# Third layer of a four-layer transformer kernel: row maxima of four heads taken in four 32-row tiles of TensorE

## The chip, the cores and the metric

The kernel runs on one core of one Trainium2 chip. Its time is the device time of one launch in microseconds (us); the lower, the better. TensorE (PE) multiplies, VectorE (DVE), ScalarE (ACT) and GpSimd (POOL) work on elements, SyncE (SP) issues the DMAs. Each engine runs its own instruction list in order; semaphores tie the lists together.

## The reference

Four layers on `x` of shape (4, 1024, 256), with a residual and a layer norm around each. The change is in the third, a causal softmax attention of 16 heads of width 16, whose output is scaled per key row by a gate:

```
Q = (x @ Wq + bq).reshape(B, S, 16, 16)        # K and V likewise
logits = einsum('bqhd,bkhd->bhqk', Q, K) * 16 ** -0.5
attn = softmax(where(causal, logits, -inf))
gate = tanh(...)                                # one number for each (b, q)
out = einsum('bhqk,bkhd->bqhd', attn * gate[:, None, None, :], V) @ Wo + bo
```

(`gate[:, None, None, :]` runs over the keys.)

## The kernel before

`layer3` treats the four sequences one after the other: `projections`, `attention`, `output`. All are unrolled, and the order of the work on each engine is the order in which the Python code emits it; nothing reorders it but the waits on semaphores.

**Layout of Q and K.** `qst` and `kst` are [128, 8, 1024]. One index of the middle axis holds two heads (`a` = 0, 1), each on 64 partitions: four blocks of 16 rows. In `qst` they hold the high part of Q, its low part, nothing, the high part; in `kst` high, high, nothing, low. One product over the 64 rows thus gives hi·hi + lo·hi + hi·lo, a score close to full precision out of fp32r operands. The first row of the empty block is special: `kst` has -1 there (`krow`), and `qst` gets the row maximum of that query, so that the same product subtracts the maximum. The layout is made by matmuls with `select` in `projections`.

**Maxima first.** The maximum of a query row over its keys is needed before its scores can be exponentiated. So `attention` computes the scores twice. A *maxima tile* (list `tiles`, 96 for each sequence) is 128 queries by up to 512 keys of both heads `a` of one sub-group `u`: `maxima_part` runs one 64-row matmul for each head (L1571) into a bank each, and, where the tile touches the diagonal, two bf16 matmuls that add the causal mask (L1574, L1576). Tiles alternate between two pairs of the four banks 4 to 7; the wait `s.max_read >= i - 1` asks that tile `i - 2` was read. VectorE reduces both banks of a tile in one instruction (L1690) into `peak`, or for queries 512 to 1023, whose keys come in two halves, into `low` and `high`, which L1696 combines. SyncE then carries each column of 128 maxima into its row of `qst` by a DMA (L1559, two for each query tile).

**Scores, exponentials, values.** 48 *steps* (`steps`; one chunk of four heads and 512 queries by one key tile of 128) follow. A step has four score matmuls (`scores_part`, L1588, with two mask matmuls L1591 and L1593 on the diagonal), in the order j=0: a=0, a=1, j=1: a=0, a=1, each into one of three banks; four exponentials on ScalarE (L1678) which free those banks; and the products with V of the step two before (`weighted`, L1606, each issued as two passes). The chunks are: 0 and 1 (queries 0 to 511, four steps each), 2 to 5 (queries 512 to 1023, eight steps each), 6 and 7 (queries 0 to 511 again). Chunk c may begin when all its maxima have landed (`shifted`).

**Which maxima when.** Twelve tiles stand ahead of the first step, with the eight V projections (`value`, L1624) between them; the others are dealt out to the steps by `tiles_to`, so that each chunk's tiles are done four tiles ahead of its first step. In a step, half of its tiles go with j=0 and half with j=1, and of the first tile of each half one head's part is emitted behind each score matmul.

```
if i >= 2:
    pe.wait_ge(s.max_read, i - 1)
at = MAX + 2 * (i % 2) + a
```

## Time and profile before

| | us |
|---|---|
| runs of the kernel, median (lowest, highest) of 3 | 3317.6 (3314.07, 3318.29) |
| the profiled execution, its own time | 3319.22 |
| span of its profile | 3317.5 |
| PE busy over the span | 3158.2 (95%) |
| DVE / ACT / POOL busy | 1831.4 / 1477.7 / 1018.0 |
| attention of the third layer, four sequences, first start to end | 148.8, 144.1, 152.5, 146.6 |

The four attentions start at 1854.4, 2059.4, 2261.4 and 2470.4 us of the span. The second one (2059.4 to 2203.5) is looked at closely, since all four have the same instructions. "Busy" of PE counts a matmul from its start to its modelled end, and matmuls overlap, so a PE that is busy need not be streaming. The page's chain of what ended last is of no help here: it only covers the fourth layer.

### The profile page before, as it was taken

The numbers are of one execution on the slowest core, as the hardware profiler recorded it, in microseconds if no ns is written. First come the engines' busy times: TensorE is split into PE (matmuls) and PEld (weight loads), VectorE is DVE, ScalarE is ACT, GpSimd is POOL, SyncE is SP. The second block draws the span as 40 slices with busy tenths as digits, with TensorE's granted clock in tenths as the row PEclk, the third lists the DMA queues.
The fourth block names the chain that finished last, engine by engine and source line by source line (L and its number), as shares of the span: only waits on it lengthen the run. The fifth ranks groups of instructions, "written<-read, shape, count | busy, mean of one in ns | idle before, by whom it ended". The sixth has DMA issues, their size and how long they took to land. (4 is left out here: it accounts for less than half of the span.)

```text
span 3317.5 us, 49554 instructions
## 1 busy us (share of the span) xinstructions
PE 3158.2 (95%) x18066; PEld 2264.4 (68%) x18066; DVE 1831.4 (55%) x3090; ACT 1477.7 (45%) x2732; POOL 1018.0 (31%) x919
## 2 busy tenths in 40 slices
PE   7999999999999999999999999999999999999998
PEld 4667656975588756986578546555465588888886
DVE  4556745775467744866464665756557433333332
ACT  3332354424542254422543574655756644444443
POOL 1224424752266423753256304022040211111110
PEclk9999999999999999999999999998999999999999
DMA  6212111011121111111121001010100300000000
GB/s 204 67 39 72 33 31 56 31 47 39 30 71 39 39 28 47 39 52 34 32 61 52 2 3 51 2 27 1 9 20 2 131 25 13 13 13 14 7 7 14
DMA packets 182673, 124.07 MB, mean 37 GB/s; under 512 B 125216, under 2 KB 163360, under 8 KB 178976
## 3 DMA queue, kind: packets, MB, share of 16 engines
q1 hardware_dynamic: 182432, 120.87, 12.9%
q8 instruction: 149, 2.44, 0.3%
q14 instruction: 92, 0.75, 0.1%
HBM read 103.37 MB, written 28.44 MB: 40 GB/s over the span
## 5 line engine op out<-in xcount | busy, mean ns | idle before, releaser
L1950 PE MATMUL sums<-l_uhi,l_h 128*128 128x512 f32 x1024 | 406.3, 397 | 0.0
L1678 ACT ACTIVATE l3b_prob<-sums 128x512 f32<-128x512 f32 (+3 forms) x768 | 333.2, 493 | 160.4 <-PE sums L1593 121.7
L1950 PE MATMUL sums<-l_ulo,l_h 128*128 128x512 f32 x1024 | 403.9, 394 | 0.0
L644 POOL TENSOR_TENSOR l_qrow<-l_vm,l_qst 128x512 fp32r<-128x512 f32 x256 | 355.6, 1406 | 146.2 <-ACT l_qst L638 145.3
L1032 DVE TENSOR_REDUCE l2b_mx<-sums 128x1 fp32r<-128x1024 f32 (+7 forms) x256 | 192.6, 758 | 255.7 <-PE sums L943 254.0
L968 PE MATMUL sums<-sb_nx,l_vx 128*128 128x512 f32 (+3 forms) x768 | 302.2, 503 | 2.1 <-ACT l_od L1008 2.1
L1588 PE MATMUL sums<-l_qst,l_kst 64*128 64x512 f32 (+3 forms) x768 | 278.2, 426 | 15.6 <-ACT l3b_prob L1678 6.3
L2037 DVE TENSOR_TENSOR l_ulo<-l_made,l_uhi 128x512 fp32r<-128x512 f32 x128 | 90.4, 706 | 362.6 <-ACT l_uhi L1969 362.6
L1001 ACT ACTIVATE sb_nx<-sums 128x512 f32<-128x512 f32 (+3 forms) x384 | 182.3, 493 | 220.7 <-PE sums L960 215.4
L638 ACT CAST l_qst<-l_vm 128x512 fp32r<-128x512 f32 x256 | 158.2, 620 | 237.7 <-DVE l_vm L631 138.6
L1571 PE MATMUL sums<-l_kst,l_qst 64*128 64x512 f32 (+3 forms) x768 | 242.2, 443 | 22.2 <-DVE l3b_low L1690 11.8
L1588 PEld LDWEIGHTS sums<-l_qst,l_kst 64*128 64x128 f32 x768 | 140.2, 195 | 154.1 <-ACT l3b_prob L1678 136.5
L631 DVE TENSOR_TENSOR l_vm<-l_oT,sums 128x512 f32<-128x512 f32 x256 | 172.4, 681 | 120.6 <-PE sums L623 119.4
L1950 PEld LDWEIGHTS sums<-l_uhi,l_h 128*128 128x128 f32 x1024 | 192.9, 188 | 44.8 <-POOL l_ulo L2105 1.3
L1950 PEld LDWEIGHTS sums<-l_ulo,l_h 128*128 128x128 f32 x1024 | 193.0, 188 | 43.4
L1239 PE MATMUL sums<-l_kst,l_qst 128*128 128x256 f32 x768 | 217.5, 283 | 0.0
L2105 POOL TENSOR_TENSOR l_ulo<-l_made,l_uhi 128x512 fp32r<-128x512 f32 x64 | 82.4, 1292 | 437.7 <-ACT l_uhi L1969 437.7
L746 PE MATMUL sums<-l_kst,l_qst 128*128 128x512 f32 x512 | 208.0, 406 | 8.0 <-PEq L1107 7.4
L1996 ACT ACTIVATE l_made<-sums,l_scale 128x512 f32<-128x512 f32 x128 | 88.2, 689 | 279.3 <-PE sums L1950 279.2
L800 DVE TENSOR_TENSOR l_vm<-sums,l_gm 128x512 f32<-128x512 f32 x256 | 174.3, 689 | 66.5 <-PE sums L746 66.0
L957 PE MATMUL sums<-l_qst,l_kst 128*128 128x512 f32 (+3 forms) x384 | 206.9, 539 | 4.0 <-issue 4.0
L746 PE MATMUL sums<-l_kst,l_qrow 128*128 128x512 f32 x512 | 200.3, 391 | 0.0
(274 smaller groups left out, 7826.4 us busy)
## 6 DMA issues: line engine op xcount, KB each, us to landing
l_ve<-ve SPq DMA_DIRECT2D x32, 512.0 KB, 4.0
l_oe<-oe SPq DMA_DIRECT2D x16, 1024.0 KB, 5.0
between<-sb_x SPq DMA_DIRECT2D x48, 256.0 KB, 2.1
l_vm<-weights_copy SPq DMA_DIRECT2D x32, 352.0 KB, 3.4
sb_nx<-between SPq DMA_DIRECT2D x9, 1024.0 KB, 5.7
weights_copy<-h SPq DMA_DIRECT2D x2, 4096.0 KB, 26.1
l_ve<-inverse SPq DMA_DIRECT2D x32, 256.0 KB, 3.6
l_qst<-l3b_peak SPq DMA_DIRECT2D x512, 0.5 KB, 2.0
```

What stands on the lines that cost most here:

```text
L644: pool.tensor_tensor(rlo[:, i % RT, :], routed[:, i % RT, :], rhi[:, i % RT, :].bitcast(F32), ALU.subtract).then_inc(s3.routed_lo, 1)
L746: last = pe.matmul(bank(m.ps, n % RING), x[:, c, t * P:(t + 1) * P], v[:, h % 2, c, :], start=(c == 0 and x is xhi and v is vhi), stop=(c ...
L800: dve.tensor_tensor(by_key(vm[:, n % VM, :]), by_key(bank(m.ps, n % RING)), gm[:, at:at + NE].unsqueeze(1).to_broadcast([P, DH0, NE]), ALU ...
L957: pe.matmul(out, kst[:, h % RK, at], qst[:, h % RK, lo:hi], start=True, stop=False)
L968: last = pe.matmul(bank(m.ps, PV, lo, hi), vx[:, k, h // 2, DH0 * (h % 2):DH0 * (h % 2) + P], prob[:, k % 2, lo:hi], start=(k == 0), stop= ...
L1001: act.activation(prob[:, k % 2, lo:hi], bank(m.ps, n % 3, 0, hi - lo), ACT.Exp, scale=SCALE0).then_inc(s.exp_ready, 1)
L1032: dve.reduce_max(mx[:, h1, t:t + 1], bank(m.ps, max_bank(h1, k1), 0, (t + 1) * P), AX_X).then_inc(s.max_read, 1)
L1239: last = pe.matmul(m.ps[:, t * D:(t + 1) * D], r[:, k % RT, cols], w(c, expert(e))[:, 0, :], start=(c == e == 0 and t % 2 == 0 and r is rh ...
L1571: last = pe.matmul(bank(m.ps, at, 0, hi - lo), qst[rows(a), p, t * P:(t + 1) * P], kst[rows(a), p, lo:hi], start=True, stop=True)
L1588: last = pe.matmul(bank(m.ps, part % SCORE, 0, hi - lo), kst[rows(a), p, k * P:(k + 1) * P], qst[rows(a), p, lo:hi], start=True, stop=True)
L1678: act.activation(prob[:, i % RB, j, a, 0:hi - lo], bank(m.ps, part % SCORE, 0, hi - lo), ACT.Exp, scale=SCALE1).then_inc(s.exp_ready, 1)
L1950: run(lambda out, a, x, first, last: pe.matmul(out, a, x, start=first, stop=last))
```

## The change

It touches the third layer only.

- **Layout.** For the odd index of the middle axis the four blocks of 16 rows are rotated by two: empty, third term, first, second. So the first two terms of an even and of an odd index lie on different 32-row quarters of each head's 64 rows (0 to 31 and 32 to 63). The special row moves with them (partition 0 instead of 32; `krow` has a column for each, `spread` writes every other index).
- **Maxima.** `maxima(i)` now does tiles `i` and `i + 1` at once, the same queries and keys of an even and an odd sub-group: four matmuls (four heads), each over the 32 rows of its quarter, into banks 4, 5, 6 and 7 together. The third term (hi·lo) is left out of the maxima; the scores still have it. The subtracted number is then only nearly the maximum, which a softmax allows.
- **Masks of the maxima.** A mask now spreads over 32 rows, so a diagonal pair of tiles takes four groups of four bf16 matmuls (128, 96, 64 and 32 columns), 16 where 8 stood.
- **Waits.** `maxima(i)` waits for `s.max_read >= i`, that is, until all four banks were read.
- **Order.** `tiles` runs over a chunk's query tiles with j innermost; `tiles_to` is rounded to even numbers; a pair is emitted as a whole behind the two score matmuls of j=0 or of j=1, no longer between them. SyncE's DMAs alternate between the two sub-groups of a chunk.
- **Loads.** The mask operands grow from 3 blocks of 256 to 2 of 256 and 2 of 512 columns for each partition, once.

```diff
-        tiles = [(u, t, lo, hi) for u, (p, n) in enumerate(subs) for t in range(TPH * n, TPH * n + TPH)
-                 for lo, hi in halves(0, (t + 1) * P)]
+        tiles = [(2 * c + j, t, lo, hi) for c, (g, n) in enumerate(chunks) for t in range(TPH * n, TPH * n + TPH)
+                 for lo, hi in halves(0, (t + 1) * P) for j in range(2)]
...
-                for u, (p, n) in enumerate(subs):
-                    if u >= 2:
-                        sp.wait_ge(shifted[u % 2], carried(u - 2))
+                for c, (g, n) in enumerate(chunks):
                     for j in range(TPH):
-                        if n:
-                            sp.wait_ge(s.combined, combined_to(u, j))
...
+                        for u in (2 * c, 2 * c + 1):
...
+                def maxima(i):
+                    _u, t, lo, hi = tiles[i]
+                    if i:
+                        pe.wait_ge(s.max_read, i)
+                    ranges = [(lo, hi, None)]
                     if hi == (t + 1) * P:
...
+                        ranges += [(hi - P + q * P // QUARTERS, hi, q) for q in range(QUARTERS)]
+                    for first, end, q in ranges:
+                        for j in range(2):
+                            p = subs[tiles[i + j][0]][0]
+                            for a in range(2):
+                                quarter = slice(R * a + R // 2 * j, R * a + R // 2 * j + R // 2)
+                                out = bank(m.ps, MAX + 2 * j + a, first - lo, end - lo)
...
-                    now = list(range(tiles_to[i], tiles_to[i + 1]))
+                    now = list(range(tiles_to[i], tiles_to[i + 1], 2))
...
                             scores_part(i, j, a)
-                            if share[j]:
-                                maxima(share[j][0], a)
...
+                        for both in share[j]:
+                            maxima(both)
```

On TensorE, the first maxima ahead of the steps: `l_kst,l_qst` is the maxima matmul, `rowmask_qk` its mask, `l_wv` a V projection. Before:

```order
L1571 MATMUL sums<-l_kst,l_qst 128x128
L1574 MATMUL sums<-l_rowmask_qk,l_rowpick 128x128
L1576 MATMUL sums<-l_rowmask_qk,l_rowpick 128x64
L1571 MATMUL sums<-l_kst,l_qst 128x128
L1574 MATMUL sums<-l_rowmask_qk,l_rowpick 128x128
L1576 MATMUL sums<-l_rowmask_qk,l_rowpick 128x64
L1624 MATMUL sums<-l_wv,l_xT 128x256 x2
```

The same place in the changed kernel (`quartermask` is the mask of a quarter):

```order
L1584 MATMUL sums<-l_kst,l_qst 128x128 x4
L1587 MATMUL sums<-l_quartermask,l_quarterpick 128x128 x4
L1587 MATMUL sums<-l_quartermask,l_quarterpick 128x96 x4
L1587 MATMUL sums<-l_quartermask,l_quarterpick 128x64 x4
L1587 MATMUL sums<-l_quartermask,l_quarterpick 128x32 x4
L1630 MATMUL sums<-l_wv,l_xT 128x256 x2
```

Two rows of heads became four, and a V projection still stands behind each two tiles. On TensorE in the first step of chunk 2, the end of the step before (`l_qst,l_kst` is a score matmul, `l3b_prob,l_vx` the product with V):

```order
L1588 MATMUL sums<-l_qst,l_kst 128x512
L1571 MATMUL sums<-l_kst,l_qst 128x512
L1574 MATMUL sums<-l_rowmask_qk,l_rowpick 128x128
L1576 MATMUL sums<-l_rowmask_qk,l_rowpick 128x64
L1588 MATMUL sums<-l_qst,l_kst 128x512
L1571 MATMUL sums<-l_kst,l_qst 128x512
L1588 MATMUL sums<-l_qst,l_kst 128x512
L1571 MATMUL sums<-l_kst,l_qst 128x512
L1606 MATMUL sums<-l3b_prob,l_vx 32x512 x4
```

The same step in the changed kernel, with the row ahead of it:

```order
L1618 MATMUL sums<-l3b_prob,l_vx 32x256 x4
L1600 MATMUL sums<-l_qst,l_kst 128x512 x2
L1584 MATMUL sums<-l_kst,l_qst 128x512 x4
L1600 MATMUL sums<-l_qst,l_kst 128x512 x2
L1618 MATMUL sums<-l3b_prob,l_vx 32x512 x4
```

The maxima no longer alternate with the scores: they stand in one block of four between the scores of j=0 and of j=1, and the step has one block of two tiles where three tiles stood. On VectorE, chunk 2's first reads (chunk indices as above), before:

```order
L1690 TENSOR_REDUCE l3b_high<-sums 128x2
L1696 TENSOR_TENSOR l3b_peak<-l3b_low,l3b_high 128x2x3
L1690 TENSOR_REDUCE l3b_low<-sums 128x2
L1690 TENSOR_REDUCE l3b_high<-sums 128x2
L1696 TENSOR_TENSOR l3b_peak<-l3b_low,l3b_high 128x2
```

and in the changed kernel:

```order
L1693 TENSOR_REDUCE l3b_high<-sums 128x2
L1699 TENSOR_TENSOR l3b_peak<-l3b_low,l3b_high 128x2x3
L1693 TENSOR_REDUCE l3b_high<-sums 128x2
L1699 TENSOR_TENSOR l3b_peak<-l3b_low,l3b_high 128x2x3
L1693 TENSOR_REDUCE l3b_low<-sums 128x2 x2
L1693 TENSOR_REDUCE l3b_high<-sums 128x2
L1699 TENSOR_TENSOR l3b_peak<-l3b_low,l3b_high 128x2
```

The reads are the same in number and size; they come in twos, and a combination of the even sub-group stands between the two reads of a pair.

## Rows read from the trace of the kernel before

**Rows 1.** By stretch: length; PE, PEld, DVE, ACT, POOL busy (count); granted clock; DMA
```profile
2059.40:2073.60 14.20, 13.22 (x104) 9.15 (x104) 9.35 (x12) 3.01 (x9) 9.82 (x12) 1.00 0.10 2
2073.60:2100.60 27.00, 24.00 (x249) 14.88 (x249) 21.84 (x27) 14.75 (x34) 7.78 (x6) 0.87 0.09 2
2100.60:2164.80 64.20, 60.57 (x584) 30.74 (x584) 48.87 (x62) 45.14 (x100) 0.00 (x0) 1.00 0.07 2
```
**Rows 2.** VectorE by line and shape, second sequence: count, busy us, mean ns, idle before
```profile
L1690 DVE TENSOR_REDUCE l3b_peak<-sums 128x2 fp32r<-128x768 f32 x8 | 7.6, 956 | 3.3 <-PE sums L1576 2.1 <-DMA l_qst<-l3b_peak 1.1
L1690 DVE TENSOR_REDUCE l3b_peak<-sums 128x2 fp32r<-128x512 f32 x8 | 5.5, 690 | 2.6 <-PE sums L1576 2.6
```
**Rows 3.** VectorE in order of time: start, length; several reads in one row where x2
```profile
2067.18 1.56 DVE L1690 TENSOR_REDUCE l3b_peak<-sums 128x2 fp32r<-128x1024 f32 x2 [0.42 <-PE sums L1576]
2069.01 2.69 DVE L1690 TENSOR_REDUCE l3b_peak<-sums 128x2 fp32r<-128x512 f32 x3 [0.27 <-PE sums L1576]
...
2096.51 1.23 DVE L1690 TENSOR_REDUCE l3b_high<-sums 128x2 f32<-128x1024 f32 x1 [0.32 <-PE sums L1576]
...
2097.85 1.22 DVE L1690 TENSOR_REDUCE l3b_low<-sums 128x2 f32<-128x1024 f32 x1
2098.99 0.42 DVE L1690 TENSOR_REDUCE l3b_high<-sums 128x2 f32<-128x256 f32 x1
```
**Rows 4.** TensorE in order of time: maxima, masks and V ahead of the steps
```profile
2065.47 1.13 PE L1624 MATMUL sums<-l_wv,l_xT 128*128 128x256 f32 x4
2066.53 0.51 PE L1571 MATMUL sums<-l_kst,l_qst 64*128 64x512 f32 x2
2066.86 0.24 PE L1574 MATMUL sums<-l_rowmask_qk,l_rowpick 64*128 64x128 bf16 x2
2066.93 0.21 PE L1576 MATMUL sums<-l_rowmask_qk,l_rowpick 64*128 64x64 bf16 x2
```
**Rows 5.** TensorE and VectorE: one maxima tile off the diagonal and its read
```profile
2131.06 0.60 PE L1571 MATMUL sums<-l_kst,l_qst 64*128 64x512 f32 x2
```
```profile
2131.85 1.23 DVE L1690 TENSOR_REDUCE l3b_low<-sums 128x2 f32<-128x1024 f32 x1 [0.45 <-PE sums L1571]
```
**Rows 6.** ScalarE in chunk 5: a step of 512 queries without maxima, then the next
```profile
2182.54 2.06 ACT L1678 ACTIVATE l3b_prob<-sums 128x512 f32<-128x512 f32 x4 [0.63 <-PE sums L1593]
2185.14 1.57 ACT L1678 ACTIVATE l3b_prob<-sums 128x512 f32<-128x512 f32 x3 [0.53 <-PE sums L1593]
```
**Rows 7.** TensorE in chunk 5: products with V, then scores
```profile
2180.92 1.06 PE L1606 MATMUL sums<-l3b_prob,l_vx 128*32 128x512 f32 x8
2181.91 0.50 PE L1588 MATMUL sums<-l_qst,l_kst 64*128 64x512 f32 x2
...
2183.73 0.85 PE L1606 MATMUL sums<-l3b_prob,l_vx 128*32 128x384 f32 x8
2184.51 0.49 PE L1588 MATMUL sums<-l_qst,l_kst 64*128 64x512 f32 x1
```
**Rows 8.** SyncE: DMAs of the maxima, 2060.0 to 2080.9, and issue to landing
```profile
2060.38 20.90 SPq L1559 DMA_DIRECT2D l_qst<-l3b_peak  x32
```
```profile
DMA to landing us min/median/max: 1.9/2.0/3.2
```
**Rows 9.** By stretch as rows 1: within chunks 0 and 1, third sequence
```profile
2275.60:2281.00 5.40, 3.90 (x47) 2.70 (x47) 4.24 (x5) 3.83 (x6) 5.20 (x6) 1.00 0.12 4
2281.00:2305.00 24.00, 23.81 (x163) 14.16 (x167) 15.84 (x21) 9.95 (x25) 2.60 (x1) 0.50 0.07 2
```
**Rows 10.** ScalarE: first exponentials of chunks 0 and 2, second and third sequence
```profile
2074.87 1.09 ACT L1678 ACTIVATE l3b_prob<-sums 128x512 f32<-128x512 f32 x2
...
2101.06 2.00 ACT L1678 ACTIVATE l3b_prob<-sums 128x512 f32<-128x512 f32 x3 [0.40 <-PE sums L1588]
...
2276.90 2.39 ACT L1678 ACTIVATE l3b_prob<-sums 128x512 f32<-128x512 f32 x4
...
2308.46 1.62 ACT L1678 ACTIVATE l3b_prob<-sums 128x512 f32<-128x512 f32 x3 [0.41 <-PE sums L1588]
```

More of the change, by code:

```diff
@@ L1375, in _ @@
                         for a in range(2):
-                            r = 2 * (j % 2) + a
-                            pe.matmul(bank(m.ps, r), select[:, kind, 0, r, :], zhi[:, i % RZ, :], start=True, stop=False)
-                            last = pe.matmul(bank(m.ps, r), select[:, kind, 1, r, :], zlo[:, i % RZ, :], start=False, stop=True)
+                            at, r = 2 * (j % 2) + a, j % 2 + 2 * a
+                            pe.matmul(bank(m.ps, at), select[:, kind, 0, r, :], zhi[:, i % RZ, :], start=True, stop=False)
+                            last = pe.matmul(bank(m.ps, at), select[:, kind, 1, r, :], zlo[:, i % RZ, :], start=False, stop=True)
                         last.then_inc(s.stack_mm, 1)
@@ L1534, in wanted @@
             return peaked[-1]
-        tiles_to = [min(max(first_pair, sum(v < wanted(x) for v in peaked)), len(tiles)) for x in scored]
+        tiles_to = [min(max(first_pair, -(-sum(v < wanted(x) for v in peaked) // 2) * 2), len(tiles)) for x in scored]
         finish_in = {steps.index((c, keys[n][-1])): c for c, (g, n) in enumerate(chunks)}
@@ L1609, in weighted @@
                     last.then_inc(s.pv_mm, 1)
-                def maxima(i, a):
-                    last = maxima_part(i, 1 - a)
-                    if a == 0:
-                        return
-                    last.then_inc(s.max_mm, 1)
                 def warm(at, a):
@@ L1629, in _ @@
                     pe.wait_ge(ld.value_in, 32)
-                for i in range(tiles_to[0]):
-                    for a in range(2):
-                        maxima(i, a)
-                    if i % 2 == 0 and i // 2 < BESIDE:
+                for i in range(0, tiles_to[0], 2):
+                    maxima(i)
+                    if i // 2 < BESIDE:
                         value(i // 2)
@@ L1643, in _ @@
                             scores_part(i, j, a)
-                            if share[j]:
-                                maxima(share[j][0], a)
-                            elif i > steps.index((len(chunks) - 1, 0)):
+                        for both in share[j]:
+                            maxima(both)
+                        if not share[j] and i > steps.index((len(chunks) - 1, 0)):
+                            for a in range(2):
                                 warm(MAX + 1 - a, 1 - a)
-                        for t in share[j][1:]:
-                            for a in range(2):
-                                maxima(t, a)
                     if i >= LAG:
@@ L2233, in layout3 @@
     for r in range(4):
+        copy = (out // DH1 % 4) ^ (2 * (r % 2))
         source = (2 * r + out // (4 * DH1)) * DH1 + out % DH1
@@ L2237, in layout3 @@
             select[source[used], kind, lo[used].astype(int), r, out[used]] = 1.0
-    krow = np.where(out % (4 * DH1) == 2 * DH1, np.float32(-1.0), np.float32(0.0)).reshape(P, 1)
-    row = np.arange(P) % HPART
-    rowpick, rowmask = np.zeros((P, 2, P), np.float32), np.zeros((P, 2, 2, P), np.float32)
-    for part in range(2):
-        rowpick[np.arange(P), part, row + HPART * part] = 1.0
-        rowmask[:, 0, part, :] = constants()["mask_qk"][row + HPART * part, :]
-        rowmask[:, 1, part, :] = constants()["mask_kq"][row + HPART * part, :]
+    krow = np.stack([np.where(out % (4 * DH1) == at, np.float32(-1.0), np.float32(0.0)) for at in (2 * DH1, 0)], 1)
+    rowpick, rowmask = [], []
+    for height, mask in ((HPART, "mask_kq"), (P // 4, "mask_qk")):
+        row = np.arange(P) % height
+        for part in range(P // height):
+            pick = np.zeros((P, P), np.float32)
+            pick[np.arange(P), row + height * part] = 1.0
+            rowpick.append(pick)
+            rowmask.append(constants()[mask][row + height * part, :])
+    rowpick, rowmask = np.stack(rowpick, 1), np.stack(rowmask, 1)
     return {
```

63 lines of the change are left out of this document (33 added, 30 removed).

## The prediction, made before the changed kernel ran

> **What bounds the kernel now.** Only the attention of the third layer changes, four times the same, so I read the second sequence and multiply by four. First the busy times by stretch [rows 1]: the stretch ahead of the steps takes 14.2 us, chunks 0 and 1 take 27.0, chunks 2 to 4 take 64.2. PE is busy for 93, 89 and 94% of them, VectorE for 66, 81 and 76%, ScalarE for less. Busy PE here is not full PE: matmuls overlap, and a wait can hide behind a modelled end. So I read a step in which nothing of the maxima stands. One of 512 queries takes 2.60 us from first exponential to first exponential, of which ScalarE works 2.06 [rows 6]; the step is a loop: score, exponential, release of a bank, last score, products with V (0.99 us from their start to the next score [rows 7]), next score. The middle of a step therefore has room, about 0.65 us, in which a maxima tile costs nothing. A whole chunk of eight steps with two tiles a step takes 21 to 22 us. What stands beside PE is VectorE: reads of 0.96 and 0.69 us for 384 and 256 keys [rows 2], 1.22 and 0.42 for 512 and 128 [rows 3]. These overlap their neighbours a little: 1.14 us from start to start behind a full read, and three reads of 256, 384 and 512 keys in 2.69 [rows 3]. It can work without gaps only because PE fills one pair of banks while VectorE empties the other. Up to chunk 4 the kernel is bound by this pipeline of PE and VectorE together, not by TensorE's arithmetic.
>
> **What a pair of tiles costs on TensorE.** Today a diagonal tile of 512 keys starts at 2066.53, its masks at 2066.86 and 2066.93 [rows 4]: about 0.43 us of PE, of which 0.33 is load and streaming of two rows of heads abreast. Two tiles: 0.86. Afterwards four rows of heads go abreast: 0.33 again, then four mask groups instead of two. The second mask group starts 0.07 behind the first [rows 4]; the narrower ones I put at 0.05 to 0.06, so some 0.23 for four. A diagonal pair takes about 0.6 instead of 0.86, one off the diagonal 0.35 instead of 0.66. Over 48 pairs of a sequence, with narrower tiles, this is 10 to 14 us less work of PE. It is only a gain where PE's own stream sets the pace.
>
> The trace prices a change of tile shape. From V products (128*32) to scores (64*128), 512 columns take 0.99 us and 384 take 0.78 [rows 7]; 0.21 for each 128 columns leaves a fixed 0.15. The changed kernel has two more changes of shape with each pair, 0.2 to 0.3 us; it eats most of the saving off the diagonal. The Trainium skill (TensorEngine Tiling (Array Packing), Key Properties) says that changing the tiling mode, not just the tile, drains TensorE; the fixed part agrees, and without that rule the PE side of each pair would be 0.2 to 0.3 cheaper.
>
> **What the new wait costs.** Here is the main term. `maxima(i)` waits until all four banks were read; before, one pair of banks was always ahead. So between the last read of one pair and the first read of the next stands: PE's restart, the matmuls, their masks and the semaphore. From the rows: diagonal, first matmul to read is 2066.53 to 2067.18, 0.65 us [rows 3, 4]; two further mask groups and four tiles instead of two add 0.19, so 0.84 for 512 keys and 0.05 less for each 128 fewer. Off the diagonal: 2131.06 to 2131.85, 0.79 with the second matmul held up by a score between them [rows 5]; abreast I take 0.65. Restart behind a read 0.05 (estimate from start and end of successive rows). In this gap VectorE idles. Reading a pair takes 2.36 us for 512 keys (1.14 + 1.22), 1.83, 1.30 and 0.76 for 384, 256 and 128. A combination between the two reads of an upper diagonal pair adds 0.2 (2096.51 to 2097.85 is 1.34, not 1.14 [rows 3]). So from pair to pair at best: 3.05 us off the diagonal; 3.25, 2.67, 2.09 and 1.49 on it, 0.2 more for the two with a combination.
>
> What is queued behind the waiting PE: the scores of j=1, the V products, the next scores; and ScalarE starves behind them, since three banks of scores are all it has.
>
> **Ahead of the steps.** Pairs of 128, 256, 384, 512, 128 and 256 keys with a V projection of 1.06 us behind each of five, three more at the end. PE waits for VectorE about 0.5, 0.9 and 1.4 us behind the second, third and fourth pair, and saves some 0.3 a pair. Sum: first score 15.3 us behind the first maxima instead of 14.2.
>
> **Chunks 0 and 1.** Twelve pairs, 24 tiles, in steps 0 to 7, nearly all of which VectorE already filled. The chain: 2.67 + 3.25 + 3.05 + 1.49 + 3.05 + 2.09 + 3.05 + 2.87 + 3.05 + 3.45 + 3.05 = 31.1, from 15.6 on, then 1.3 to the first score of chunk 2: 48.0 us behind the first maxima, instead of 41.1. So **+6.9 us** by here, the 1.1 ahead of the steps included.
>
> **Chunks 2 to 4.** Chunk 2: one pair a step: four at 3.05, then 2.09, 2.87, 3.45, and the pair of 128 keys, behind which PE's own work rules (2.2): 22.8; and 0.5 for the DMAs. These are issued every 0.65 us, and land 2.0 later [rows 8]; SyncE has twelve at once behind the last but one pair of a chunk, four behind the last, which puts the landing close to the chunk's start. Chunk 3: seven pairs, and behind the last a step without one (4.7 to the next pair): 22.3. Chunk 4: nine pairs, two in some steps: 22.6, and 0.45 for the DMAs. Together 68.6 instead of 64.2: **+4.4 us**.
>
> **Chunks 5 to 7.** Few pairs, mostly in the room of a step; some gain in 5 and 6, one loss where two pairs share a step: -0.1.
>
> **Sum of the waits:** 11.2 us a sequence, 45 in all. The mask operands' longer copies are on ScalarE under the last matmuls of the first projections: nothing, 0.1 to 0.9 us once if they stick out. The projections have the same instructions.
>
> **The clock.** In the third sequence the granted clock was 0.50, the lower level of 1.2 GHz, for 24 us in chunks 0 and 1 [rows 9], and these took 31.6 us, where the second's took 26.2 [rows 10] with a mean of 0.87 [rows 1]. That is 5.4 us for some 17 us more at the lower level, 0.32 for each. Ahead of that fall PE was busy for 3.90 of 5.40 us [rows 9]; the change adds idle time of PE of that kind. I put 10 us more of it in a sequence: +3, 12 in all. From nothing to 40 us more: 0 to 13 a sequence.
>
> **Sum.** The profiled execution took 3319.2 us, span 3317.5; the median of the runs is 1.6 less. 3319.2 + 45 + 12 = 3376, on the scale of the median **3374 us**, 1.7% slower.
>
> **Rivals.**
> (a) *TensorE's stream is what counts*, and the waits for VectorE fall into the steps' room. Then the 10 to 14 us of PE work come back from each sequence: 40 to 55 us less, about 3270. For it: PE is 93% busy, and a quarter of its maxima work goes. Against it: a step without any maxima still takes 2.60 us, and a single gap of 3.05 us is longer than that. It decides if the gap between reads is under about 0.5 us instead of 0.7 to 0.9. Beside it the Trainium skill (TensorE: Matmul & The Clock Gate, Measured speedup vs the span model) gives four row tiles 3.07 times the speed of one after another; by that, too, PE's own work would shrink as in this case.
> (b) *Four quarters don't run abreast*, only two at a time: each pair takes 0.2 us more before its read. With 42 pairs up to chunk 4: +8.4 a sequence, about 3408.
> (c) *The clock stays low* through chunks 0 to 4 for most of the time: +10 a sequence on the 3, about 3414.
> (d) *A draw*: gaps 0.15 us shorter than mine (-6 a sequence), slots with slack elsewhere that the shorter maxima fill (-5). About 3320. It would also look so if the change did not make the waits that its code shows.
>
> A lower bound for the case forecast: if PE never kept VectorE waiting otherwise, the pairs up to chunk 4 would add up to 111.0 us instead of 105.4, +5.6 a sequence; with gaps 0.1 us shorter, +1.4. That is 3323. The upper one is (c).
>
> **Chances.** Forecast 0.62, (c) 0.14, (b) 0.08, (a) 0.12, (d) 0.04. What a measurement of this kernel can tell from no change is about 0.2%, 6.6 us. Range 3325 to 3420: it holds the forecast with its bounds, (b) and (c), and leaves (a) and (d) out. Slower 0.84, within 0.2% 0.04, faster 0.12.
>
> **What would show it.** Right: on VectorE, behind every second read an idle stretch of 0.6 to 0.9 us that ends on the maxima or their last mask; starts of pairs off the diagonal 3.0 to 3.1 us apart in chunk 2; chunks 0 and 1 longer by about 6 us, chunks 2 to 4 by about 4, chunks 5 to 7 the same; a maxima matmul of TensorE waiting for the second read of the pair before. Wrong: four maxima matmuls that start one after another by more than 0.1 us (then b); a first read within 0.5 us of its matmuls (then a or d); a step time of 2.6 us in chunk 2. And if PE's idle time ends on ScalarE rather than on VectorE, the maxima are not the bound that I take them for.

## The result and the profile after

The changed kernel takes **3422.15 us** (median of 4 runs, 3419.88 to 3430.66) where the kernel before takes 3315.84 beside it (4 runs, 3313.93 to 3318.29): a ratio of 1.0313, 95% interval 1.0297 to 1.0330, so 3.1% slower. The forecast was 3374, range 3325 to 3420. The sign was right; the measured loss of 106 us is nearly twice the 57 us foretold, and the median lies 2 us above the range.

The profiled execution took 3421.58 us with a span of 3419.9, which is 102.4 more than before's. The four attentions of the third layer hold nearly all of it. Their windows in the changed kernel, each from the first maxima matmul to the end of the last exponential (up to 2.3 us shorter than the lengths in the table of the kernel before, which end later); the columns are stretch and length, busy time of PE, PEld, DVE, ACT, POOL (with counts), granted clock of PE, DMA share, GB/s:

```profile
1853.80:2028.90 175.10, 150.54 (x1564) 71.78 (x1568) 93.55 (x128) 90.44 (x208) 17.55 (x17) 0.80 0.08 8
2087.70:2256.30 168.60, 147.83 (x1564) 69.97 (x1568) 93.54 (x128) 90.14 (x208) 17.51 (x17) 0.80 0.08 8
2314.80:2488.60 173.80, 148.85 (x1564) 71.59 (x1568) 93.55 (x128) 90.37 (x208) 17.56 (x17) 0.80 0.08 8
2547.10:2715.60 168.50, 144.34 (x1563) 69.92 (x1567) 93.56 (x128) 90.03 (x208) 17.55 (x17) 0.83 0.08 8
```

and the same view of the kernel before:

```profile
1854.40:2000.90 146.50, 137.30 (x1312) 75.84 (x1316) 93.91 (x128) 91.08 (x208) 17.61 (x17) 0.95 0.10 9
2059.40:2203.30 143.90, 134.56 (x1312) 74.35 (x1316) 93.92 (x128) 90.89 (x208) 17.61 (x17) 0.98 0.10 9
2261.50:2412.20 150.70, 141.32 (x1312) 78.43 (x1316) 94.11 (x128) 91.20 (x208) 17.59 (x17) 0.91 0.10 9
2470.40:2615.30 144.90, 136.11 (x1312) 75.35 (x1316) 93.92 (x128) 90.77 (x208) 17.60 (x17) 0.96 0.10 9
```

The sums are 686.0 and 586.0 us: 100 us. Beside the length, the clock column moved most. Since it has two levels, 1.00 and 0.50, a stretch spent twice its length times (1.00 less the mean) at the lower one: 70 of the first 175.1 us. Over the four, from the records behind these rounded means, it is 266 us after and 58 before. VectorE's and ScalarE's work is what it was.

Two mechanisms of the forecast are plain to see. First, PE now waits for VectorE. The line of the maxima matmuls in the changed kernel, and what ended the idle time ahead of them (us, times). The list adds up the idle time of the matmuls (PE) and of the weight loads (PEld), which run side by side:

```profile
L1584 PE MATMUL sums<-l_kst,l_qst x768: 293/491/792, 1853.7 to 2700.0; 32*128 32x512 f32 x96, 32*128 32x128 f32 x32, 32*128 32x256 f32 x32, 32*128 32x384 f32 x32
  DVE l3b_high L1693: 91.9, 83
  DVE l3b_peak L1693: 65.6, 62
  DVE l3b_low L1693: 31.8, 52
```

That is 189 us for both; the same three reads ended 64 us of it before, when the maxima matmuls stood in L1571:

```profile
  DVE l3b_low L1690: 37.8, 74
  DVE l3b_peak L1690: 20.3, 43
  DVE l3b_high L1690: 6.3, 14
```

Of the matmuls alone it is 80.0 us after (39.1, 27.1 and 13.8 for `high`, `peak` and `low`) and 19.5 before.

Second, VectorE is idle between two pairs, as it was not in [rows 3]. PE and then VectorE of the changed kernel, at full clock (start, duration, engine, line, operation, count, and in brackets the idle time before and what ended it):

```profile
2183.60 0.51 PE L1584 MATMUL sums<-l_kst,l_qst 32*128 32x512 f32 x4
2183.94 0.33 PE L1587 MATMUL sums<-l_quartermask,l_quarterpick 32*128 32x128 bf16 x16
2184.20 0.49 PE L1600 MATMUL sums<-l_qst,l_kst 64*128 64x384 f32 x2
...
2186.93 0.51 PE L1584 MATMUL sums<-l_kst,l_qst 32*128 32x512 f32 x4 [1.12 <-DVE l3b_high L1693]
2187.37 0.50 PE L1600 MATMUL sums<-l_qst,l_kst 64*128 64x512 f32 x2
```

```profile
2184.32 1.23 DVE L1693 TENSOR_REDUCE l3b_high<-sums 128x2 f32<-128x1024 f32 x1 [1.52 <-PE sums L1587]
2185.58 0.16 DVE L1699 TENSOR_TENSOR l3b_peak<-l3b_low,l3b_high 128x2 fp32r<-128x2 f32 x1
2185.66 1.22 DVE L1693 TENSOR_REDUCE l3b_high<-sums 128x2 f32<-128x1024 f32 x1
2186.91 0.16 DVE L1699 TENSOR_TENSOR l3b_peak<-l3b_low,l3b_high 128x2 fp32r<-128x2 f32 x1
2187.47 1.23 DVE L1693 TENSOR_REDUCE l3b_low<-sums 128x2 f32<-128x1024 f32 x1 [0.40 <-PE sums L1584]
```

From the first matmul of a pair to its first read stand 0.54 us off the diagonal (2186.93 to 2187.47) and 0.72 on it (2183.60 to 2184.32). Where nothing else comes between two pairs, VectorE's idle stretch at full clock is 0.59 to 0.79 us; the 0.40 above follows a combination, and in the 1.52 PE was at the scores, their masks and the V products. The four tiles are over in 0.51 us, one tile's time, so four heads do go abreast. The first reads of the two pairs start 3.15 us apart.

### The profile page after: what moved, and what is told of

Read it like the earlier page. It is cut to its first block and busy times, and to the rows that moved or that the text cites. A ratio compares the mean times of both kernels' runs of the same rounds, so it can differ in the third digit from the quotient of the medians.

```text
span 3419.9 us, 51603 instructions
## 1 busy us (share of the span) xinstructions
PE 3204.3 (94%) x19090; PEld 2246.1 (66%) x19090; DVE 1831.4 (54%) x3090; ACT 1474.1 (43%) x2733; POOL 1017.7 (30%) x919
## 3 DMA queue, kind: packets, MB, share of 16 engines
q1 hardware_dynamic: 182432, 121.27, 12.5%
## 5 line engine op out<-in xcount | busy, mean ns | idle before, releaser
L1600 PE MATMUL sums<-l_qst,l_kst 64*128 64x512 f32 (+3 forms) x768 | 232.9, 504 | 13.0 <-ACT l3b_prob L1681 9.9
L1600 PEld LDWEIGHTS sums<-l_qst,l_kst 64*128 64x128 f32 x768 | 108.6, 214 | 195.4 <-ACT l3b_prob L1681 135.2
L149 POOL TENSOR_SCALAR sb_nx<-sb_nx,sb_moments,sb_rstd 128x256 f32<-128x256 f32 x32 | 38.5, 1219 | 610.9 <-DVE sb_rstd L120 610.9
```

What stands on the lines that cost most here:

```text
L1600: last = pe.matmul(bank(m.ps, part % SCORE, 0, hi - lo), kst[rows(a), p, k * P:(k + 1) * P], qst[rows(a), p, lo:hi], start=True, stop=True)
```

## Where the time lies: chunks at either clock

I cut each attention at the first exponential of each chunk, as in [rows 10]. In microseconds, with the time at the lower clock in brackets:

| | before, sequences 1 to 4 | after, sequences 1 to 4 |
|---|---|---|
| ahead of the steps | 15.4 | 18.6 (7), 15.6, 18.5 (7), 18.4 (7) |
| chunk 0 | 14.1 (7), 14.0 (7), 16.2 (12), 15.2 (10) | 16.8 (10), 18.1 (17), 16.8 (10), 16.8 (10) |
| chunk 1 | 12.2, 12.2, 15.4 (12), 12.1 | 19.2 (17), 19.5 (19), 19.1 (17), 20.1 (20) |
| chunk 2 | 21.0, 21.0, 20.7, 21.0 | 22.2 (0), 28.0 (22), 22.2 (0), 27.2 (18) |
| chunk 3 | 21.3 | 23.6 (3), 23.0 (3), 23.6 (3), 23.0 (3) |
| chunk 4 | 22.0 | 27.5 (10), 26.0 (7), 27.6 (10), 24.6 (0) |
| chunk 5 | 19.8 | 25.5 (15), 20.1 (0), 23.8 (10), 20.2 (0) |
| chunk 6 | 9.9 | 12.9 (9), 9.5, 9.5, 9.5 |
| chunk 7 | 10.8 (7), 8.3, 10.2 (3), 8.3 | 8.7, 8.7, 12.7 (10), 8.7 |

One kernel, one chunk, the same instructions, and two durations: chunk 2 as windows, in sequences 1 to 4 (the clock is the third column from the end):

```profile
1908.40:1930.60 22.20, 18.24 (x229) 8.30 (x228) 16.33 (x20) 15.15 (x34) 0.00 (x0) 1.00 0.06 2
2141.00:2168.90 27.90, 26.66 (x228) 10.54 (x228) 16.32 (x20) 15.25 (x33) 0.00 (x0) 0.61 0.05 2
2369.30:2391.50 22.20, 18.22 (x229) 8.30 (x228) 16.32 (x20) 15.14 (x34) 0.00 (x0) 1.00 0.06 3
2602.40:2629.60 27.20, 25.32 (x228) 10.14 (x228) 16.32 (x20) 15.29 (x33) 0.00 (x0) 0.67 0.05 2
```

and chunk 5 in the first and second sequence:

```profile
1981.70:2007.20 25.50, 24.32 (x216) 10.24 (x216) 6.43 (x9) 15.09 (x33) 0.00 (x0) 0.71 0.08 2
2218.00:2238.00 20.00, 18.29 (x216) 8.37 (x216) 6.36 (x9) 14.74 (x33) 0.00 (x0) 1.00 0.09 3
```

This prices the lower clock: 5.7 us for 22, 5.0 for 18, 5.5 for 15; between 0.26 and 0.37 us for each microsecond spent low. The other cells of the changed kernel's column that have a full-clock neighbour in their row go from 0.21 (chunk 4) to 0.45 (ahead of the steps), and over all twelve it is 43 us for 132, or 0.33. (The forecast had 0.32 from one such pair in the kernel before.) The Trainium skill (TensorE: Matmul & The Clock Gate, Terms) puts the penalty at the throttled time times one less K/N, which is 0.5 at 1.2 GHz; here it is less. Probably that is so because VectorE or ScalarE holds up PE part of the time anyway; no run separates this. With 0.33, the 208 us more at the lower clock are some 69 of the 100 us. The rest, some 31, are waits and the order of the work.

## The experiments

Each kernel is given with its median and, as a ratio, against runs of the kernel before on the same chip. The medians come from several chips, on which the kernel before took 3316 to 3322 us, so differences between kernels go by the ratios. "Attentions" and "low" are the length of the four attentions and the time at the lower clock in them, in the one profiled execution.

| kernel | us | ratio [95%] | attentions | low |
|---|---|---|---|---|
| before | 3315.84 | 1 | 586 | 58 |
| after | 3422.15 | 1.0313 [1.0297, 1.0330] | 686 | 266 |
| before_onebuf | 3552.35 | 1.0712 [1.0676, 1.0749] | 806 | 351 |
| after_split | 3459.35 | 1.0438 [1.0394, 1.0482] | 714 | 372 |
| after_fill | 3477.15 | 1.0458 [1.0420, 1.0497] | 751 | 201 |
| before_fill | 3341.71 | 1.0070 [1.0042, 1.0098] | 601 | 14 |
| wide_order | 3334.19 | 1.0035 [1.0018, 1.0052] | 607 | 99 |
| wide_onebuf | 3394.32 | 1.0216 [1.0195, 1.0236] | 661 | 154 |
| before_half | 3270.69 | 0.9854 [0.9830, 0.9878] | 533 | 0 |
| after_half | 3370.74 | 1.0149 [1.0119, 1.0178] | 628 | 239 |
| wide_half | 3329.63 | 1.0027 [1.0013, 1.0041] | 590 | 68 |
| after_widemask | 3436.42 | 1.0366 [1.0332, 1.0400] | 692 | 290 |
| before_fewfill | 3313.45 | 0.9981 [0.9971, 0.9991] | 578 | 24 |

One execution's low time could be chance. But every execution has its mean granted clock on record, over the whole kernel, and the kernels that are compared below don't overlap in it: 0.930 to 0.940 for after_split and 0.979 to 0.987 for wide_order; 0.950 to 0.957 for the kernel after and 0.973 to 0.976 for wide_onebuf; 0.955 to 0.960 for after_half and 0.979 to 0.986 for wide_half.

### First round: the wait and the clock

The theory of the forecast was the wait for all four banks; its rival, the clock. Four kernels: that wait put into the kernel before; the wait split in the kernel after; and idle matmuls (results unused) that keep PE busy, in both.

**before_onebuf**, the kernel before with a wait for all four banks:

```
-                        pe.wait_ge(s.max_read, i - 1)
+                        pe.wait_ge(s.max_read, i - i % 2)
```

> The kernel before, with one edit: the maxima wait until all four banks were read (for an even tile), so no pair of banks is ahead of VectorE. 64-row tiles, third term, order and masks are those of before. Theory W (the wait is the cause, with the lower clock that PE's idle time brings): 60 to 110 us slower than before, 3375 to 3425 us, and a mean clock near that of the changed kernel (0.956). Rival S (the 32-row shape costs: changes of shape, four mask groups, quarters that don't run abreast): at most 15 us slower, up to 3330 us, clock 0.98 to 0.99.

Measured: 3552.35 us (3543.97 to 3563.95), +234, far above the 60 to 110 expected. The wait alone can cost more than the whole change; but this kernel interleaves the two heads of a tile with the scores (first head behind one score matmul, second behind the next) and doesn't hand out its tiles in twos, so the parts of a pair are spread over several score matmuls, and the wait stands among them. It bounds nothing for the kernel after, which emits a pair in one place. Why it is 234 and not, say, 100, these runs don't separate; 293 us more at the lower clock are some 97 of it at 0.33. Its maxima are all 64 rows high, so long waits alone bring the lower clock too: 351 us of it, more than in the kernel after. The cleaner form of this test is wide_onebuf, below.

**after_split**, the kernel after with one sub-group's two heads behind the other's, each pair of banks with its own wait:

```
-                    if i:
-                        pe.wait_ge(s.max_read, i)
...
-                    for first, end, q in ranges:
-                        for j in range(2):
+                    for j in range(2):
+                        if i:
+                            pe.wait_ge(s.max_read, i - 1 + j)
+                        for first, end, q in ranges:
```

> The changed kernel, with its layout, order and 32-row tiles, but each tile of a pair waits only for the read of its own two banks, and the two tiles of a pair are issued one after the other (two quarters abreast, not four). Theory W: VectorE is fed ahead again, 3300 to 3335 us, mean clock 0.98 or more. Rival S: the 32-row matmuls, the mask groups and the changes of shape are all still there, so 3390 us or more.

Measured: 3459.35 us (3451.21 to 3477.45), slower still. **The theory that the wait is the whole loss fell here.** With the old wait back the time should have come down; instead the clock went lower. Windows of its first two attentions:

```profile
1853.70:2045.10 191.40, 185.71 (x1556) 88.98 (x1556) 93.00 (x128) 91.70 (x208) 17.56 (x17) 0.66 0.07 7
2104.20:2263.40 159.20, 150.46 (x1564) 76.46 (x1568) 92.90 (x128) 90.74 (x208) 17.60 (x17) 0.87 0.09 9
```

372 of 714 us are at the lower clock. PE is busy for 97 and 94.5% of these two (before: 94%), but that can't be read by itself, since a lower clock makes matmuls longer and PE busier. So I read one fall, in the third attention, the 3.4 us ahead of it and the 37.5 behind:

```profile
2348.80:2352.20 3.40, 3.17 (x48) 1.89 (x50) 2.96 (x5) 1.32 (x4) 0.00 (x0) 1.00 0.00 0
2352.20:2389.70 37.50, 36.98 (x282) 16.88 (x280) 21.90 (x28) 16.08 (x38) 0.00 (x0) 0.50 0.05 2
```

At full clock PE was busy for 3.17 of 3.40 us, and the clock fell all the same; ahead of the fall of [rows 9] it was 3.90 of 5.40. But this fall is no proof that the 32-row tiles bring it. The clock had been low just before as well (2338.5 to 2348.8). And the kernel before has a fall of the same kind, at 1990.9 in its first attention, five microseconds behind its last maxima; ahead of it PE was busy for 3.09 of 3.40 us, with scores and V products only:

```profile
1987.50:1990.90 3.40, 3.09 (x34) 1.76 (x30) 0.00 (x0) 2.14 (x6) 0.00 (x0) 1.00 0.29 40
```

Nor does the clock come back when the 32-row tiles end. In the first attention of after_split the last of them is over at 2021.9, and the clock stays low to the attention's end with PE busy throughout:

```profile
2022.00:2045.00 23.00, 23.00 (x138) 10.52 (x138) 5.09 (x18) 10.77 (x28) 0.00 (x0) 0.50 0.17 47
```

What the height does is read from pairs of kernels that differ in it, in the next two rounds.

**after_fill** and **before_fill** put three idle 128x512 matmuls ahead of the maxima. The kernel after has them at every pair up to the second step and then at the pairs that go with j=0; the kernel before has them in steps 0 to 7 (chunks 0 and 1) only. The core of the edit, here that of after_fill:

```
+                def fill(at, n=3):
+                    for _ in range(n):
+                        pe.matmul(bank(m.ps, at), select[:, 0, 0, 0, :], select[:, 0, 0, :, :], start=True, stop=True)
...
+                            if i < LAG:
+                                fill(PV)
+                            elif j == 0:
+                                pe.wait_ge(s.exp_ready, 4 * i + 2 - SCORE + 1)
+                                fill((4 * i + 2) % SCORE)
```

> The changed kernel with three idle matmuls of 512 columns ahead of a pair of maxima (all pairs ahead of the steps, and those that go with j=0), into a bank that nobody reads then; they fill the time in which TensorE waits for VectorE's read. Theory W with the clock as its second half: most of the 208 us more at the lower clock go, the mean clock rises to 0.975 or more, and 35 to 60 us come back: 3360 to 3390 us. Rival C (the clock falls for another reason, such as the 32-row matmuls themselves): clock stays below 0.965 and the time is 3415 us or more.

> The kernel before with the same idle matmuls at the maxima of chunks 0 and 1 alone, where its own clock fell (58 us at the lower level over the four attentions). If idle time of TensorE there is what the clock falls on: 3300 to 3312 us, clock 0.99. If the idle matmuls stand in the way of work: 3316 us or more.

Measured: 3477.15 us (3461.71 to 3494.27) and 3341.71 (3340.49 to 3346.04). The fillers raise the clock (266 to 201 us low, 58 to 14), but they cost more than they bring: after_fill loses 48 us on the kernel after by the ratios (1.0458 against 1.0313). Three of them seem to last longer than the wait they stand in, and from the third step on they also wait for ScalarE to free a bank; the two weren't separated. In before_fill chunk 0 takes 18.1 us with none of it low, where the kernel before takes 14.1 with 7 low. So this was a poor remedy. As a test it was inconclusive: the time of after_fill fits its rival expectation (3415 us or more), while its mean clock, 0.965 to 0.974, lies between the two.

### Second round: order, wait and height taken apart

The change does three things: another order of tiles (a pair in one place, upper and lower sub-group alternating), one wait for four banks, and 32 rows instead of 64. Between before and after I put two kernels with 64 rows, the third term and two mask groups: **wide_order** has only the new order, **wide_onebuf** the new wait too.

wide_order against before, the core:

```
-        tiles = [(u, t, lo, hi) for u, (p, n) in enumerate(subs) for t in range(TPH * n, TPH * n + TPH)
-                 for lo, hi in halves(0, (t + 1) * P)]
+        tiles = [(2 * c + j, t, lo, hi) for c, (g, n) in enumerate(chunks) for t in range(TPH * n, TPH * n + TPH)
+                 for lo, hi in halves(0, (t + 1) * P) for j in range(2)]
...
+                        if i and SPLIT and part is None:
+                            pe.wait_ge(s.max_read, i - 1 + j)
```

> The kernel before (64-row tiles, third term, its layout and its two mask groups) with the changed kernel's order alone: tiles in twos, a pair as one block behind the scores of j=0 or j=1, even counts, alternating DMAs; each tile waits for its own two banks, as before. It differs from after_split only in the height of the maxima's tiles. Theory O (the order costs, whatever the rows): as slow as after_split, 3430 us or more. Theory S (32-row matmuls cost, through the clock above all): 3320 to 3350 us, less than 120 us at the lower clock in the four attentions (after_split had 372).

wide_onebuf against wide_order (with it `pe.wait_ge(s.max_read, i)` stands ahead of the pair, and the four heads' matmuls directly behind one another):

```
-                    SPLIT = True
+                    SPLIT = False
```

> The same, but a pair waits until all four banks were read, as in the changed kernel; it differs from the changed kernel only in the height of the tiles (and their masks and third term). If four quarters abreast are a gain under this wait: 20 to 70 us slower than the changed kernel, 3440 to 3490 us. If 32-row matmuls cost: faster than the changed kernel's 3422. The difference to wide_order is the wait alone; theory W expects 40 to 110 us.

Measured: 3334.19 us (3325.47 to 3346.71) and 3394.32 (3390.44 to 3396.53). Both lie where the theory that the 32 rows cost through the clock put them, and the wait's 60 us lie within the 40 to 110 expected. One attention of each:

```profile
2065.40:2211.30 145.90, 132.84 (x1308) 70.20 (x1311) 92.82 (x128) 89.99 (x208) 17.64 (x17) 0.96 0.10 9
```

```profile
2077.30:2244.00 166.70, 140.93 (x1308) 71.32 (x1312) 93.58 (x128) 90.25 (x208) 17.56 (x17) 0.88 0.09 8
```

By the ratios, the steps from before to after are +0.35% for the order (12 us), +1.81% for the wait (60 us), +0.97% for the 32 rows with their masks (32 us): 104 of the 106. The wait is the largest part, but the last step is the surprise. The quarters were to save PE work and cost nothing else. At full clock they lose nothing and save a little: chunk 4 took 24.6 us in the kernel after and 24.8 in wide_onebuf,

```profile
2652.60:2677.20 24.60, 20.39 (x260) 9.53 (x260) 16.01 (x22) 14.82 (x33) 0.00 (x0) 1.00 0.06 2
```

```profile
2627.80:2652.60 24.80, 21.10 (x210) 9.93 (x208) 15.92 (x22) 14.78 (x34) 0.00 (x0) 1.00 0.06 2
```

chunk 5 took 20.1 and 20.2, chunk 6 9.5 and 9.6, and ahead of the steps the quarters save 0.9 us (15.6 and 16.5). So these 32 us come from the clock: 112 us more at the lower level.

The largest difference that the height makes is between **after_split and wide_order**. Both have the new order, and in both each tile waits for its own two banks and the two tiles of a pair go one after the other; they differ in the height of the maxima's tiles, with what belongs to it (masks, third term). after_split takes 1.0438 against 1.0035 and is 372 us low against 99. Idle time of PE can hardly be the reason here, since the kernel with 32 rows has less of it. Chunk 3 at full clock, after_split first and then wide_order, leaves PE 1.0 and 1.4 us idle:

```profile
2178.70:2200.10 21.40, 20.37 (x205) 9.06 (x204) 15.39 (x18) 15.05 (x33) 0.00 (x0) 1.00 0.07 2
```

```profile
2129.10:2149.20 20.10, 18.75 (x186) 8.74 (x182) 15.39 (x18) 15.09 (x33) 0.00 (x0) 1.00 0.06 2
```

**before_half, after_half** and later **wide_half** let VectorE read half the columns of each maxima tile, so that PE waits for it much less. The numbers subtracted are then not the maxima over all keys; these kernels are for measuring only:

```
-                    dve.reduce_max(out, max_pair(i)[:, :, 0:hi - lo], AX_X).then_inc(s.max_read, 1)
+                    dve.reduce_max(out, max_pair(i)[:, :, 0:(hi - lo) // 2], AX_X).then_inc(s.max_read, 1)
```

> The kernel before, where VectorE reads only the first half of the columns of each maxima tile, so the maxima are not those of all keys; its reads take about half the time. Tells what VectorE's reads hold up: if PE and VectorE bound chunks 0 to 4 together, 3270 to 3300 us; if PE's own stream does, within 10 us of before.

> The changed kernel with the same halved reads (same part left out). Theory W: the gap between two pairs' reads stays, the reads halve, so it gains more than the kernel before does: 3330 to 3370 us, and it ends 40 to 80 us behind before_half. Rival (TensorE's stream bounds, and the quarters save some of it): level with before_half or faster, if its clock is as high.

Measured: 3270.69 us (3269.03 to 3279.28) and 3370.74 (3361.59 to 3377.78). Halved reads take 1.5% off the kernel before and 1.6% off the kernel after, so the 100 us between the two stay. before_half came out as expected; after_half was to end 40 to 80 us behind it and ended 100 behind. The wait for the reads is now a small part: the maxima matmuls of after_half wait for VectorE for 18.3 us in all, where those of the kernel after wait for 80.0. The clock is the larger part. before_half is at 1.00 throughout, after_half still 239 us low, which at 0.33 is 79 of the 95 us between their attentions:

```profile
1855.00:1988.00 133.00, 126.24 (x1297) 70.17 (x1296) 57.54 (x128) 89.03 (x206) 17.62 (x17) 1.00 0.11 10
```

```profile
2067.70:2230.70 163.00, 153.42 (x1564) 72.68 (x1568) 55.18 (x128) 90.37 (x208) 17.42 (x17) 0.76 0.09 8
2289.20:2438.30 149.10, 137.57 (x1564) 68.09 (x1568) 55.16 (x128) 90.03 (x208) 17.42 (x17) 0.87 0.10 9
```

(The first row is before_half, the other two after_half.)

### Third round: height without waits, masks, and a remedy

**wide_half** is wide_onebuf with halved reads: the order, the wait and the small load on VectorE of after_half, but 64 rows. Its one edit is the line above.

> wide_onebuf (64-row tiles, the changed kernel's order and its wait for all four banks) with VectorE's reads halved, as in after_half: the two differ only in the height of the maxima's tiles with their masks. after_half was at the lower clock for 239 us of the four attentions, though its waits for VectorE were short. Theory S2 (32-row matmuls bring the lower clock): at most 60 us at the lower level here, 3290 to 3320 us. Rival I (idle time under the one wait brings it, whatever the rows): about 200 us at the lower level and 3350 us or more.

Measured: 3329.63 us (3320.88 to 3342.09, 10 runs), 41 us below after_half, with 68 us low instead of 239. The theory of the height had expected at most 60 us low and 3290 to 3320 us, the rival of idle time about 200 and 3350 or more: the height comes out nearer, but the order and the wait still cost 57 us here (1.0027 against before_half's 0.9854), 22 of them by the clock. Two of its attentions:

```profile
1854.10:1998.90 144.80, 129.14 (x1308) 69.50 (x1312) 55.13 (x128) 89.66 (x208) 17.49 (x17) 0.96 0.10 9
2057.90:2205.30 147.40, 132.41 (x1308) 70.47 (x1312) 55.13 (x128) 89.83 (x208) 17.53 (x17) 0.94 0.10 9
```

So with order, waits and reads alike, the height makes the difference in the clock: 0.96 and 0.94 here, 0.76 and 0.87 in the rows of after_half. 171 us low at 0.33 are 56 us; the attentions differ by 38, as the quarters save some PE work in return. More idle time is not the reason here either: the maxima matmuls wait for VectorE for 18.3 us in after_half and 22.6 in wide_half. Together with after_split and wide_order this is the best evidence that the height costs through the clock. It doesn't say how. The 32-row tiles fill fewer rows of the array, two abreast 64 of 128; they also bring changes of tile shape between maxima and scores, which 64-row maxima don't have, and they leave the third term out. No run separates these.

**after_widemask** tells the products from the many small masks. It has the products in quarters but puts the mask on over 64 rows, eight small matmuls a pair instead of sixteen:

```
-                    ranges = [(lo, hi, None)]
-                    if hi == (t + 1) * P:
-                        ranges += [(hi - P + q * P // QUARTERS, hi, q) for q in range(QUARTERS)]
...
+                    parts = [None, 0, 1] if hi == (t + 1) * P else [None]
...
+                                    last = pe.matmul(bank(m.ps, at, hi - lo - P + part * HPART, hi - lo), rowpick[rows(a), part, :],
+                                                     rowmask_qk[rows(a), part, part * HPART:P], start=False, stop=True,
+                                                     skip_group_check=True)
```

> The changed kernel, with its four quarters abreast for the products, but the masks of the maxima as two groups of 64-row matmuls, as before. If the sixteen small 32-row mask matmuls bring the lower clock: at most 160 us of it in the four attentions (the changed kernel has 266) and 3375 to 3400 us. If the 32-row products do: 230 us or more at the lower level and 3410 to 3440 us.

Measured: 3436.42 us (3425.61 to 3457.14), ratio 1.0366 [1.0332, 1.0400] against after's 1.0313 [1.0297, 1.0330]; 290 us low. Not better, a little worse. So the sixteen small masks are not the cause; the 32-row products are what is left, as the expectation has it, with the changes of shape around them. A part of the small loss may be the change of height between products and masks, which was not measured by itself.

**before_fewfill** is the kernel before with seven idle matmuls in each attention, only where its own clock fell (ahead of tiles 14, 17 and 18):

```
+                def fill(tile):
+                    for _ in range({14: 1, 17: 4, 18: 2}.get(tile, 0)):
+                        pe.matmul(bank(m.ps, PV), select[:, 0, 0, 0, :], select[:, 0, 0, :, :], start=True, stop=True)
```

> The kernel before with seven idle matmuls of 512 columns in each attention, placed only where its trace shows TensorE waiting in steps 0 and 1 (ahead of three tiles). If that idle time is what its clock falls on: less than 25 us at the lower level instead of 58, and 3302 to 3312 us. If the idle matmuls delay the work by what the clock gives back: 3314 to 3322 us.

Measured: 3313.45 us (3308.24 to 3321.18, 12 runs), ratio 0.9981 [0.9971, 0.9991]; 24 us low instead of 58. The low time is as expected; the time is just above the 3302 to 3312 us of the hopeful case. Its first attention ran wholly at full clock, in 142.3 us instead of 146.5:

```profile
1851.90:1994.20 142.30, 134.12 (x1319) 74.18 (x1323) 93.80 (x128) 90.49 (x208) 17.64 (x17) 1.00 0.10 9
2052.80:2198.70 145.90, 137.55 (x1319) 75.74 (x1323) 93.89 (x128) 91.03 (x208) 17.64 (x17) 0.96 0.10 9
```

This is the fastest complete kernel of the study, by about 0.2%: at the edge of what is worth having, but it shows that idle matmuls can pay where they fit into a wait.

## Why the prediction was right and where it fell short

**The sum, from the profiled attentions** (us; the clock column is the difference of the lows at 0.33 each, the last one what remains):

| step | attentions | of it clock | of it waits and work |
|---|---|---|---|
| order (before to wide_order) | +21 | 41 low: 14 | +7 |
| wait for four banks (to wide_onebuf) | +54 | 55 low: 18 | +36 |
| 32 rows and their masks (to after) | +25 | 112 low: 37 | -12 |
| together | +100 | 208 low: 69 | +31 |
| forecast | +57 | 12 | +45 |

With a price of 0.26 to 0.37 the clock's part is 54 to 77, and the waits' 46 to 23. The single profiles scatter too: wide_order's profiled execution is 12.5 us above its median, before's 3.4, so the order's row is too high here (12 us by the ratios).

- **Waits: right in kind; in size 36 for the wait by itself, 31 with order and height, where 45 was forecast.** The single gaps were taken too long: 0.54 against 0.65 us off the diagonal, 0.72 against 0.84 on it. So chunk 2 took 22.2 us at full clock, not the 23.3 forecast (eight pairs, 0.11 each). Chunk 3, at 23.0 with 3 us low, is some 22 at full clock, as forecast. Chunk 4 took 24.6 where 23.05 was forecast, and this excess has nothing to do with the wait: wide_order takes 23.6 to 23.9 there at full clock, too, 1.7 more than the kernel before. The forecast gave the new order no term. It costs in chunk 4 and gives back in chunks 2 and 3 (20.1 us each in wide_order's second attention, against 21.0 and 21.3); its mechanism I have not traced. That chunks 2 to 4 together come out at +4.5 us, almost the forecast's +4.4, is luck: gaps too long and an order left out cancel. Chunks 5 to 7 came out at +0.3, -0.4 and +0.4: forecast -0.1. Chunks 0 and 1 were to take 5.8 us more; they took 8.8 more in the mean, with 18 us more of the lower clock in them, which leaves about 3.
- **Ahead of the steps:** forecast +1.1; found +0.2 at full clock, +3.1 with the lower clock in it.
- **The saved PE work** is real (-12 for the height), but most of the forecast's 40 to 55 us lies in waits, as forecast. With it, 64-row and 32-row tiles are even at full clock in chunks 4 to 7, and ahead of the steps the quarters are 0.9 us shorter.
- **The clock: the step that failed.** The forecast put 10 us more of the lower clock in a sequence, with a bound of 40; it was 52. The price for each microsecond, 0.32, held (0.33); the quantity was wrong. It was put as if the clock answered to idle time of PE alone. The waits brought 55 us in all, near the expected 40. But the height brought 112 more, and the order 41 in its one profile; nothing in the kernel before, whose maxima are all 64 rows high, could show what the height does. The kernel before did show that idle time is not all: its clock also fell where PE had been busy for 3.09 of 3.40 us. An unknown whose only evidence is a single fall should have had a wider bound above, and the range with it; its top missed by 2 us.
- **Rivals.** (a) PE's stream as the bound is refuted: less work, and 106 us more. (b) Two abreast only is refuted by the rows of L1584: four within 0.51 us. (d) Draw: refuted. (c), the clock low through most of chunks 0 to 4, was at 3414 the nearest number. Its picture is right in part: the clock was low for 27 to 36 of the 36 to 38 us of chunks 0 and 1, for most of chunk 2 in two of four sequences, and for some of the time up to chunk 7.
- **Signs named ahead.** The idle stretch of VectorE, the wait of PE for the second read, chunks 5 to 7 hardly moved at full clock: as said. Chunks 0 and 1 longer "by about 6" were 9.7, 11.4, 4.3 and 9.6 us longer, which is where the clock shows most. The DMAs of the maxima land as in [rows 8], after 1.9 us at least and 2.0 in the median.

**Still open:** why 32-row maxima bring the lower clock (the runs show that they do, not whether by the rows they leave empty, by the changes of shape or otherwise); why the clock also falls with PE busy and no maxima near; why before_onebuf costs as much as it does; why the new order loses in chunk 4 what it gains in chunks 2 and 3.

## What to carry to other kernels

Packing more tiles into TensorE at once also asks for more banks at once. When four tiles abreast take all the banks that the maxima have, the double buffering is gone, and the saved matmul time comes back as a wait of the reader (60 us here, its share of the clock included, against a gain of about 12). Compare the clock column as well as the busy one: smaller tiles of the array can come with half the clock for much of the time, so cost such an edit with the low-clock time as a term of its own and with a wide upper bound. And where a clock falls in a known wait, a few idle matmuls that fit into the wait can pay; more than fit cost more than they bring.

## What the runs showed of the hardware

- At the same order and waits, maxima in 32-row tiles bring far more of TensorE's lower clock (1.2 GHz) than in 64-row tiles: 372 us against 99 over the four attentions (after_split, wide_order), with less idle time of PE at full clock (1.0 against 1.4 us in chunk 3); 239 against 68 with halved reads (after_half, wide_half).
- A nearly busy PE doesn't keep the clock up: it fell with PE busy for 3.09 of the 3.40 us before (the kernel before, 64-row maxima) and for 3.17 of 3.40 (after_split), and then stayed at 1.2 GHz for 37.5 us with PE busy for 36.98 of them.
- Long waits bring the lower clock with 64-row tiles, too: 351 us in before_onebuf.
- Two quarters abreast were worse for the clock than four: 372 us low against 266, although the former had a wait for two banks only.
- Four 32-row matmuls of 512 columns take 0.51 us together, and at full clock a chunk takes as long with them as with 64-row tiles (20.1 and 20.2, 24.6 and 24.8 us).
- The lower clock costs 0.21 to 0.45 us for each microsecond in this mixed pipeline, 0.33 over all.
